# A two-layer cross-attention and FFN kernel on one core: its table of steps is put in another order

## The chip, the core and the metric

One core of a Trainium2 chip. The metric is the device time of one execution in microseconds (us), lower is better. The core has a matrix engine (TensorE, PE in the profile; PEld is its weight load), a vector engine (VectorE, DVE), an activation engine (ScalarE, ACT), a general engine (GpSimd, POOL) and an engine that only issues transfers here (SyncE, SP). Each runs its own instruction stream in order; they meet in semaphores.

## The reference

A batch of 2 sequences of 512 rows and 128 columns goes through four residual steps. Stage 0 and stage 2 are cross-attention to 77 context rows with 16 heads of 8 columns, stage 1 is an FFN with a small low-rank term chosen by expert, stage 3 a mixture of 8 experts (each row goes through one of them).

```python
x = x + xcond(layernorm(x), ctx, tau, delta, L0 weights)   # stage 0
x = x + lora_ffn(layernorm(x), L0 weights)                 # stage 1
x = x + xcond(layernorm(x), ctx, tau, delta, L1 weights)   # stage 2
x = x + switch_ffn(layernorm(x), L1 weights)               # stage 3

# xcond:  q = x@Wq.T+bq; k = ctx@Wk.T+bk; v = ctx@Wv.T+bv
#         a = softmax((q k * tau + delta)/sqrt(8)); out = (a v) @ Wo.T + bo
# lora_ffn: e = argmax(x@gate_W.T+gate_b)
#         out = relu(x@wi_W.T + wi_b + (x@A[e].T)@B[e].T) @ wo_W.T + wo_b
# switch_ffn: p = softmax(x@sw+sb); e = argmax p
#         out = (gelu(x@w1[e]+b1[e]) @ w2[e] + b2[e]) * p[e]
```

## The kernel before

Everything is in float32 and stays on the chip; 128 rows make a tile, so a batch has four tiles. The work is cut into some 280 named steps. `schedule()` holds one table of them; each engine's program is made by walking this same table and emitting that engine's share of each step, so the table alone sets the order on every engine. A step is `kind/layer/batch/number` (or `kind/stage/batch` for the four layer norms); `a:b` after the last number means from a to b-1. The kinds that matter here:

- `ln` and `xn`: layer norm statistics (VectorE L591, L594; ScalarE L494, L497) and the normalised rows `XN` (VectorE L603). `xt`: TensorE transposes them (L821), ScalarE copies them to `XNT` (L501), GpSimd adds a bias row to `X` meanwhile (L460).
- `kp/l`: the keys of layer l for both batches. TensorE L831 (8 instructions in the trace), ScalarE L509 and L516 (`Kf`, `Kt`), VectorE L625 (a copy `Ks<-Kt` that rounds) and L627. `km/l/b`: the masked copy `KG` of the keys, by VectorE for (0,0), by GpSimd L453 otherwise.
- `vp/l/b/j`: value projection, one matmul (L842, two instructions in the trace) and one VectorE operation (L643, `VP`).
- `q/l/b/g`: queries of head group g: TensorE L849, ScalarE L521, VectorE L648 (`QG`). `max/l/b/i`: TensorE L866 and a VectorE maximum L657 (`MR`). `mt/l/b/half`: the maxima are transposed (L875) and go into `QG` (ScalarE L526, VectorE L663). `sc/l/b/t`: scores, TensorE L891, exponential on ScalarE L534 (`P`, three buffers). `pv/l/b/t`: probabilities by values, TensorE L910. `on`, `ot`, `wo`: division, transposition and output projection (VectorE L670 and L675; TensorE L920, ScalarE L538; TensorE L927, VectorE L684).
- FFN 0: `gate/b` (TensorE L940, then on VectorE the six operations L695 to L706 and `U`, L715), `ut/b` (TensorE L948, VectorE L732 and L733; for b = 0 before them L728 and L729, which make `LS` from `LB`), `hid/b/0..3` (TensorE L953 and L957; the relu is on ScalarE L543 for even, on VectorE L738 for odd numbers), `out/b` (TensorE L967, VectorE L684).
- Stage 3: `route/b` and `prob/b` (TensorE L940, VectorE L695 to L708, ScalarE L548, VectorE L720 and L722), `rank/b` and `tiles/b` (TensorE L977 and L982, VectorE L747 to L765). After `rank/b` GpSimd scatters the four tiles of rows by expert to `slots` in HBM (L468), which needs the result of `rank` (`slot_ready`) and of `prob` (`p_ready`); SyncE then loads them back as `XS`. `moe/t` is the pipeline over 22 sorted tiles (11 of each batch): transposition of tile t+1 (L1004), first matmul of tile t (L1011), second of tile t-2 (L1022).

Two more things hold the steps together. The results of `xt`, `kp`, `q`, `vp`, `max`, `mt`, `gate` and others share four PSUM banks, given out in turn by `banks()` in the order of the table; a step waits for the reader of the bank's previous use. And GpSimd, which walks the same table, has little to do: it clears and fills constants for stage 3 where it meets `km/1/0`, which in both tables comes right after its part of `xt/1/0` in its own order:

```python
def moe_constants():
    finish(pool.memset(XS[:, :, :], 0.0), blank)              # L435
    ...
for s in steps:
    if s == ("km", 1, 0):
        moe_constants()
    if s[0] == "km" and s != ("km", 0, 0):
        pool.wait_ge(k_split, l + 1)                          # after L627 of kp/l
        ...
        for odd in (0, 1):
            finish(pool.tensor_tensor(*masked_k(b, odd), ALU.mult), kg_pool)
```

Of the kernel before, what the change touches and what calls it, by code (L numbers as in the profile page):

```python
# [96 lines left out]
def schedule():  # L97

    table = """
        ln/0/0 xn/0/0 delta xt/0/0 kp/0 q/0/0/0 km/0/0 q/0/0/1:4 max/0/0/0:3 km/0/1 vp/0/0/0 max/0/0/3:8 vp/0/0/1:4
        mt/0/0/0 vp/0/0/4 max/0/0/8 sc/0/0/0 ln/0/1 xn/0/1 max/0/0/9:11 pv/0/0/0 sc/0/0/1 max/0/0/11 vp/0/1/0 pv/0/0/1
        xt/0/1 sc/0/0/2 max/0/0/12 sc/0/0/3 vp/0/1/1 q/0/1/0 max/0/0/13:15 pv/0/0/2:4 max/0/0/15 sc/0/0/4 mt/0/0/1
        pv/0/0/4 max/0/1/0 vp/0/1/2 sc/0/0/5 max/0/1/1 q/0/1/1 vp/0/1/3 q/0/1/2 max/0/1/2:4 pv/0/0/5 vp/0/1/4  # L110
        max/0/1/4 sc/0/0/6 max/0/1/5 sc/0/0/7 q/0/1/3 pv/0/0/6:8 sc/0/0/8 max/0/1/6 sc/0/0/9 pv/0/0/8 max/0/1/7:10
        pv/0/0/9 on/0/0 mt/0/1/0 ot/0/0 sc/0/1/0 max/0/1/10:14 sc/0/1/1 wo/0/0 max/0/1/14 pv/0/1/0 sc/0/1/2 ln/1/0
        pv/0/1/1 vp/1/0/0 sc/0/1/3 xn/1/0 max/0/1/15 kp/1 pv/0/1/2 xt/1/0 mt/0/1/1 sc/0/1/4 gate/0 vp/1/0/1:3
        pv/0/1/3:5 sc/0/1/5:7 ut/0 pv/0/1/5 vp/1/0/3 hid/0/0:2 vp/1/0/4 hid/0/2 sc/0/1/7 hid/0/3 pv/0/1/6 vp/1/1/0
        out/0 vp/1/1/1 km/1/0 sc/0/1/8 pv/0/1/7 sc/0/1/9 ln/2/0 xn/2/0 pv/0/1/8:10 xt/2/0 vp/1/1/2 on/0/1 q/1/0/0:2
        vp/1/1/3 max/1/0/0:2 q/1/0/2 ot/0/1 max/1/0/2:7 wo/0/1 max/1/0/7 vp/1/1/4 ln/1/1 xn/1/1 mt/1/0/0 q/1/0/3
        xt/1/1 max/1/0/8 sc/1/0/0:2 max/1/0/9:11 gate/1 pv/1/0/0 max/1/0/11 pv/1/0/1 max/1/0/12:14 ut/1 max/1/0/14:16
        sc/1/0/2 hid/1/0 km/1/1 sc/1/0/3 hid/1/1:4 pv/1/0/2 mt/1/0/1 out/1 sc/1/0/4 pv/1/0/3 sc/1/0/5 pv/1/0/4 ln/2/1
        sc/1/0/6 xn/2/1 pv/1/0/5 sc/1/0/7 xt/2/1 pv/1/0/6 q/1/1/0:3 sc/1/0/8 max/1/1/0 pv/1/0/7 max/1/1/1:4 sc/1/0/9
        pv/1/0/8 max/1/1/4:8 pv/1/0/9 on/1/0 mt/1/1/0 max/1/1/8:10 q/1/1/3 sc/1/1/0 ot/1/0 max/1/1/10 pv/1/1/0 wo/1/0  # L120
        sc/1/1/1 max/1/1/11:14 sc/1/1/2 max/1/1/14 pv/1/1/1 sc/1/1/3 max/1/1/15 pv/1/1/2 mt/1/1/1 pv/1/1/3 sc/1/1/4:6
        ln/3/0 xn/3/0 pv/1/1/4 sc/1/1/6 pv/1/1/5 sc/1/1/7 xt/3/0 route/0 prob/0 pv/1/1/6:8 sc/1/1/8 rank/0 sc/1/1/9
        tiles/0 pv/1/1/8:10 on/1/1 ot/1/1 wo/1/1 ln/3/1 xn/3/1 moe/-1 xt/3/1 moe/0 route/1 moe/1 rank/1 tiles/1 prob/1
    """
# [984 lines left out]
```

## Time and profile before

| | before |
|---|---|
| time, median of 3 executions | 224.57 us (222.85 to 227.26) |
| span of the profiled execution, first to last instruction | 223.3 us |
| PE busy | 180.6 us (81%) |
| DVE busy | 140.4 us (63%) |
| ACT busy | 93.1 us (42%) |
| POOL busy | 62.9 us (28%) |
| mean granted TensorE clock | 0.908 of full speed |

The span is that of one profiled execution and is 1.3 us under the median of the unprofiled ones. Busy times are of instructions on the engine; an engine that is idle waits for a semaphore or issues. The granted clock is TensorE's clock as a share of 2.4 GHz; 0.5 is its lower level, 1.2 GHz. Times within the span count from its first instruction.

### The profile page before, as it was taken

How to read it: one execution, taken by the hardware profiler on the slowest of the kernel's cores; microseconds unless marked ns; L12 is line 12 of the kernel's file. 1: busy time of each engine (PE TensorE's matmuls, PEld its weight loads, DVE VectorE, ACT ScalarE, POOL GpSimd, SP SyncE). 2: the span in 40 equal slices, each digit the busy share in tenths (PEclk: the TensorE clock that was granted, in tenths of full speed). 3: DMA queues.
4: the chain of work that ended last, by engine and by line, in shares of the span. 5: the costliest groups of instructions: out<-in, count | busy, mean ns of one | idle time of the engine just before them, and what ended most of it. 6: DMA issues, size and time to landing. Idle time of an engine off the chain costs nothing.

```text
span 223.3 us, 3676 instructions
## 1 busy us (share of the span) xinstructions
PE 180.6 (81%) x1157; PEld 150.3 (67%) x1157; DVE 140.4 (63%) x385; ACT 93.1 (42%) x180; POOL 62.9 (28%) x68
## 2 busy tenths in 40 slices
...
DMA packets 11983, 15.43 MB, mean 69 GB/s; under 512 B 1713, under 2 KB 8898, under 8 KB 11965
## 3 DMA queue, kind: packets, MB, share of 16 engines
...
q8 instruction: 10, 0.16, 0.3%
...
## 4 chain that ended last, share of the span: by engine, by line
PE 42%; DVE 15%; issue 6%; ACT 4%; DMA 2%; POOL 2%; another core or an unknown queue 1%; DVEq 0%; ACTq 0%; POOLq 0%
PE scores L1011 8%; PE acc L1022 7%; PE acc L910 6%; PE shared L953 3%; PE shared L967 3%; PE shared L849 3%; DVE Ks L625 2%; PE scores L891 2%; PE shared L866 2%; PE shared L940 2%; DVE XN L603 2%; PE shared L821 1%; PE shared L1004 1%; DMA slots<-ROW,slot 1%; DVE stats L591 1%
## 5 line engine op out<-in xcount | busy, mean ns | idle before, releaser
L910 PE MATMUL acc<-VP,P 123*128 123x128 f32 (+1 forms) x320 | 42.9, 281 | 2.0 <-ACT P L534 2.0
L910 PEld LDWEIGHTS acc<-VP,P 123*128 123x128 f32 (+1 forms) x320 | 40.5, 195 | 5.2 <-ACT P L534 2.8
L534 ACT ACTIVATE P<-scores 123x512 f32<-123x512 f32 (+1 forms) x40 | 23.2, 595 | 36.5 <-PE scores L891 36.5
L460 POOL TENSOR_TENSOR X<-X,ROWS 128x512 f32<-128x512 f32 x6 | 8.1, 1352 | 86.2 <-DVE XN L603 86.1
L657 DVE TENSOR_REDUCE MR<-shared 128x4 f32<-128x308 f32 x64 | 27.1, 471 | 4.4 <-PE shared L866 3.8
L1011 PE MATMUL scores<-XST,HT 128*128 128x128 f32 x176 | 26.9, 303 | 3.4 <-ACT XST L564 3.4
L1011 PEld LDWEIGHTS scores<-XST,HT 128*128 128x128 f32 x176 | 24.7, 216 | 4.2 <-ACT XST L564 3.9
L474 POOL DMA_INDIRECT out<-XS,token x22 | 21.4, 974 | 20.1 <-DVE XS L789 17.2
L779 DVE TENSOR_TENSOR HT<-scores,B 128x512 f32<-128x512 f32 x22 | 15.2, 692 | 15.7 <-PE scores L1011 13.2
L1022 PE MATMUL acc<-W,HT 128*128 x176 | 24.9, 289 | 0.2 <-DVE XS L789 0.2
L866 PE MATMUL shared<-KG,QG 98*128 98x308 f32 x64 | 20.6, 384 | 5.1 <-DVE QG L648 4.0
L1022 PEld LDWEIGHTS acc<-W,HT 128*128 128x128 f32 x176 | 23.0, 205 | 0.4 <-issue 0.4
L891 PE MATMUL scores<-QG,KG 102*123 102x512 f32 (+1 forms) x48 | 19.6, 446 | 3.2 <-issue 2.9
L468 POOL DMA_INDIRECT slots<-ROW,slot x8 | 8.0, 1002 | 46.5 <-issue 46.5
L569 ACT ACTIVATE HT<-HT 128x512 f32<-128x512 f32 x22 | 13.9, 630 | 14.5 <-DVE HT L779 7.5
L866 PEld LDWEIGHTS shared<-KG,QG 98*128 98x128 f32 x64 | 12.0, 201 | 10.1 <-DVE QG L648 6.2
L648 DVE SCALAR_TENSOR_TENSOR QG<-shared,ATT,QG 32x512 fp32r<-32x512 f32 x16 | 11.8, 747 | 8.8 <-ACT QG L521 8.3
L849 PE MATMUL shared<-XNT,ATT 128*96 128x512 f32 x32 | 16.0, 615 | 0.9 <-issue 0.5
L562 ACT ACTIVATE HT<-W 128x512 f32 x22 | 13.8, 629 | 1.3 <-issue 1.0
L521 ACT ACTIVATE QG<-shared,ATT 96x512 fp32r<-96x512 f32 x16 | 10.8, 682 | 7.3 <-PE shared L849 7.3
L526 ACT ACTIVATE QG<-shared 6x512 fp32r<-6x512 f32 x8 | 4.7, 585 | 17.5 <-PE shared L875 17.5
L891 PEld LDWEIGHTS scores<-QG,KG 102*123 102x123 f32 (+1 forms) x48 | 8.3, 186 | 5.4 <-issue 3.6
...
## 6 DMA issues: line engine op xcount, KB each, us to landing
...
```

The source lines that it names most:

```text
L474: pool.indirect_dma_start(out, bass.IndirectOffsetOnAxis(ap=token[:, t:t + 1], axis=0), XS[:, t, 0:D], None, bounds_check=B * S - 1, oob_i ...
L534: act.activation(P[0:w, n % NP], scores[n % 2][0:w, :], ACT.Exp).then_inc(probs_ready, 1)
L562: act.activation(W1C[:, n % 2], W1[:, bass.ds(expert * F, F)], ACT.Identity).then_inc(w1_ready, 1)
L569: act.activation(HG1[:, t % NHB], HB[:, t % 2], ACT.Gelu_apprx_tanh).then_inc(gelu_ready, 1)
L657: dve.tensor_reduce(MR[:, b, qt, g, 2:2 + HG], bank(s)[:, 0:GK].rearrange("p (h k) -> p h k", h=HG), AX.X, ALU.max).then_inc(max_read, 1)
L779: dve.tensor_tensor(HB[:, t % 2].rearrange("p (k n) -> p k n", k=NF), hidden[t % 2][:, :].rearrange("p (k n) -> p k n", k=NF), bias, ALU.a ...
L849: pe.matmul(bank(s)[0:QR, :], ATT[l][:, A_Q + QR * g:A_Q + QR * (g + 1)], XNT[:, b], start=True, stop=True).then_inc(full[use[s][0]], 1)
L866: pe.matmul(bank(s)[:, 0:GK], QG[0:ONES + 2, b, g, 128 * qt:128 * qt + 128], KG[0:ONES + 2, b, g, off:off + GK], start=True, stop=True).th ...
L891: ins = pe.matmul(scores[n % 2][0:w, :], KG[:, b, g, c:c + w], QG[:, b, g], start=(i == 0), stop=(i == len(parts) - 1))
L910: ins = pe.matmul(acc[qt // 2][:, c:c + VW], P[0:w, n % NP, 128 * qt:128 * qt + 128], VP[0:w, l, b, j, half], start=(t == 0 and qt % 2 == ...
L1011: ins = pe.matmul(hidden[t % 2][:, 128 * k:128 * (k + 1)], W1C[:, t % 2, 128 * k:128 * (k + 1)], XST[:, t % 2], start=True, stop=True)
L1022: ins = pe.matmul(acc[n % 2][:, 0:D], HG1[:, n % NHB, 128 * k:128 * (k + 1)], W2[:, bass.ds(expert[n] * (NF * D) + D * k, D)], start=(k == ...
```

## The change

Only the table in `schedule()` is different. The set of steps, their instructions and all sizes are the same; what each engine does first and what later is not. Two of its lines, from the middle and the end:

```diff
-        pv/0/1/3:5 sc/0/1/5:7 ut/0 pv/0/1/5 vp/1/0/3 hid/0/0:2 vp/1/0/4 hid/0/2 sc/0/1/7 hid/0/3 pv/0/1/6 vp/1/1/0
+        sc/0/1/4 mt/0/1/1 vp/1/0/3 sc/0/1/5 gate/0 pv/0/1/4 vp/1/0/4 sc/0/1/6 pv/0/1/5 sc/0/1/7:9 ut/0 kp/1 hid/0/0:4
...
-        tiles/0 pv/1/1/8:10 on/1/1 ot/1/1 wo/1/1 ln/3/1 xn/3/1 moe/-1 xt/3/1 moe/0 route/1 moe/1 rank/1 tiles/1 prob/1
+        moe/-1 xn/3/1 xt/3/1 route/1 prob/1 moe/0:2 rank/1 tiles/1
```

What moves: `vp/0/0/0` and `kp/0` stand ahead of `xt/0/0`; `km/0/1` comes after `xt/0/1`; the value projections of batch 1 and of layer 1 come earlier; `kp/1` goes from between `xn/1/0` and `xt/1/0` to after `ut/0`; `ot/0/0` has seven steps between itself and `on/0/0`, where it had one; `wo/0/1` comes two maxima and one query step earlier; `out/1` is followed by fewer score and value steps; `km/1/1` comes after `xt/2/1`; `xt/3/0`, `route/0` and `rank/0` come earlier among the value steps; `route/1` and `prob/1` come ahead of `moe/0`.

The names of an instruction's row are output <- inputs. In the changed file every line number is one higher.

VectorE, FFN 0 of batch 0, from the normalised rows of stage 1 (`XN`) on, before:

```order
L603 TENSOR_SCALAR XN<-X,mean_var,rstd 128x128 x4
L657 TENSOR_REDUCE MR<-shared 128x4
L625 CAST Ks<-Kt 96x616
L627 TENSOR_TENSOR Ks<-Kt,Ks 32x616
L663 CAST QG<-shared 6x512
L695 TENSOR_TENSOR lg<-shared,ROWS 128x32
L696 TENSOR_REDUCE lmax<-lg 128x4
L698 TENSOR_TENSOR eq<-lg,lmax 128x32
```

The same place in the changed kernel. Ahead of the first row shown stand `XN`, two maxima, two value operations with `L664 CAST QG` between them, and the first two operations of the gate (`lg`, `lmax`):

```order
L699 TENSOR_TENSOR eq<-lg,lmax 128x32
L704 TENSOR_TENSOR eq<-eq,CON 128x32
L705 TENSOR_REDUCE first<-eq 128x4
L707 TENSOR_TENSOR hot<-eq,first 128x32
L716 TENSOR_TENSOR U<-shared,hot 128x4x32 x3
L644 TENSOR_TENSOR VP<-shared,CON 123x2x8x8
L729 CAST LS<-LB 96x512
L730 TENSOR_TENSOR LS<-LB,LS 32x512
L733 CAST U<-shared 96x512
L734 TENSOR_TENSOR U<-shared,U 32x512
L626 CAST Ks<-Kt 96x616
L628 TENSOR_TENSOR Ks<-Kt,Ks 32x616
```

The rounding copy `Ks<-Kt` stood two rows behind `XN`, ahead of the gate; it now stands behind the whole gate and the `U` work, right ahead of the odd relus of `hid`.

TensorE, FFN 0 of batch 1, from `out/1` (`W,HT`) to the queries (`XNT,ATT`) of layer 1, before:

```order
L967 MATMUL shared<-W,HT 128x128 x16
L891 MATMUL scores<-QG,KG 123x512
L910 MATMUL acc<-VP,P 128x128 x4
L891 MATMUL scores<-QG,KG 123x512
L910 MATMUL acc<-VP,P 128x128 x4
L891 MATMUL scores<-QG,KG 123x512
L910 MATMUL acc<-VP,P 128x128 x4
L891 MATMUL scores<-QG,KG 124x512 x2
L821 MATMUL shared<-CON,XN 128x128 x4
L910 MATMUL acc<-VP,P 128x128 x4
L849 MATMUL shared<-XNT,ATT 96x512 x3
```

The same place in the changed kernel:

```order
L968 MATMUL shared<-W,HT 128x128 x16
L892 MATMUL scores<-QG,KG 123x512
L911 MATMUL acc<-VP,P 128x128 x4
L892 MATMUL scores<-QG,KG 123x512
L892 MATMUL scores<-QG,KG 124x512 x2
L911 MATMUL acc<-VP,P 128x128 x4
L822 MATMUL shared<-CON,XN 128x128 x4
L892 MATMUL scores<-QG,KG 123x512
L850 MATMUL shared<-XNT,ATT 96x512 x3
```

Between `out/1` and the transposition stand two value steps (x4) where there were three and one score step fewer; between the transposition and the queries stands one score step where a value step was.

VectorE, the routing of batch 1, before, from the last operations of `rank/1` over `tiles/1` to `prob/1` (`esum`, and the reciprocal into `ROW`):

```order
L754 TENSOR_TENSOR place<-place,hot 128x32
L755 TENSOR_REDUCE slot_f<-place 128x4
L756 TENSOR_SCALAR slot<-slot_f 128x4
L761 TENSOR_TENSOR end_tile<-first_tile,tiles_of 1x8
L763 TENSOR_TENSOR past<-CON,end_tile 1x88
L764 TENSOR_REDUCE tile_f<-past 1x11
L765 TENSOR_SCALAR tile_e<-tile_f 1x11
L720 TENSOR_REDUCE esum<-ex 128x4
L722 RECIPROCAL ROW<-esum 128x4
```

In the changed kernel, from the end of `route/1` (`hotb`) over `prob/1` to the bias addition (`HT<-scores,B`) of `moe/0`, which is followed by that of `moe/1` and by `rank/1`:

```order
L709 CAST hotb<-hot 128x32
L721 TENSOR_REDUCE esum<-ex 128x4
L723 RECIPROCAL ROW<-esum 128x4
L774 TENSOR_LOAD tile_e
L774 ISA x2
L780 ISA
L780 TENSOR_TENSOR HT<-scores,B 128x512
```

`prob/1` stood last of all, behind `tiles/1`; it now stands right behind `route/1`, and both are ahead of the work on the first sorted tile.

## Rows read from the trace of the kernel before

**Rows 1.** Windows: length, busy PE, PEld, DVE, ACT, POOL (x), clock, DMA, GB/s.
```profile
57.72:86.80 29.08, 22.31 (x142) 18.67 (x140) 17.96 (x37) 7.37 (x15) 9.89 (x9) 0.88 0.31 101
62.80:69.00 6.20, 0.74 (x4) 0.33 (x3) 5.90 (x14) 1.08 (x2) 4.86 (x7) 0.79 0.67 228
69.00:73.60 4.60, 4.60 (x17) 3.77 (x18) 2.92 (x7) 0.00 (x0) 0.00 (x0) 0.54 1.07 329
...
160.90:172.00 11.10, 10.70 (x53) 10.22 (x54) 5.23 (x24) 8.69 (x15) 0.00 (x0) 0.50 0.36 116
```
**Rows 2.** Timeline of POOL: start, us, engine, line, instruction, shapes, count.
```profile
58.70 4.87 POOL L435 MEMSET XS<- 128x5720 f32 x1
...
65.50 2.57 POOL L453 TENSOR_TENSOR KG<-Ks,CON 102x616 fp32r<-102x616 f32 x2
```
**Rows 3.** Timeline of DVE, start of the kernel and FFN 0 of batch 0.
```profile
12.72 0.48 DVE L625 CAST Ks<-Kt 96x616 fp32r<-96x616 f32 x1 [0.64 <-ACT Kt L516]
...
14.84 2.70 DVE L633 TENSOR_TENSOR KG<-Ks,CON 102x616 fp32r<-102x616 f32 x2
...
56.12 1.11 DVE L603 TENSOR_SCALAR XN<-X,mean_var,rstd 128x128 f32<-128x128 f32 x4 [0.24 <-ACT rstd L497]
...
58.89 5.00 DVE L625 CAST Ks<-Kt 96x616 fp32r<-96x616 f32 x1 [1.27 <-ACT Kt L516]
63.93 0.79 DVE L627 TENSOR_TENSOR Ks<-Kt,Ks 32x616 fp32r<-32x616 f32 x1
...
65.92 0.86 DVE L698 TENSOR_TENSOR eq<-lg,lmax 128x32 f32<-128x32 f32 x1
66.81 0.19 DVE L703 TENSOR_TENSOR eq<-eq,CON 128x32 f32<-128x32 f32 x1
...
77.84 0.75 DVE L738 TENSOR_SCALAR HT<-shared,W 128x512 f32<-128x512 f32 x1 [1.92 <-PE shared L957]
```
**Rows 4.** Timeline of ACT, the keys of layer 1.
```profile
56.56 1.22 ACT L509 ACTIVATE Kf<-shared,ATT 96x154 f32<-96x154 f32 x4
57.86 1.00 ACT L516 ACTIVATE Kt<-Kf,tau 96x308 f32<-96x308 f32 x2
```
**Rows 5.** Timeline of PE, `ot/0/0` and the keys of layer 1.
```profile
49.92 0.63 PE L920 MATMUL shared<-CON,ON 128*128 128x128 f32 x4 [1.10 <-DVE ON L675]
...
55.77 1.22 PE L831 MATMUL shared<-CTX,ATT 128*96 128x154 f32 x8
```
**Rows 6.** Chain that ended last, in order of time: start, us, engine, output, line.
```profile
75.16 0.86 PE shared L953 x2
76.02 0.23 PE shared L957
76.25 0.46 PE scores L891 x2
...
77.80 0.89 PE acc L910 x8
...
78.92 3.65 PE shared L967 x32
...
86.80 0.63 PE shared L821 x4
...
114.24 3.59 PE shared L967 x32
...
121.86 0.63 PE shared L821 x4
```
**Rows 7.** Timeline of DVE, end of `rank/1` and of `prob/1`.
```profile
170.35 0.17 DVE L756 TENSOR_SCALAR slot<-slot_f 128x4 int32<-128x4 f32 x1
...
171.43 0.18 DVE L722 RECIPROCAL ROW<-esum 128x4 f32<-128x4 f32 x1
```
**Rows 8.** Timeline, `route/1` on ACT and the first scatter of batch 1 on POOL.
```profile
165.91 1.28 ACT L548 ACT_TABLE_LOAD   x1
...
172.85 0.97 POOL L468 DMA_INDIRECT slots<-ROW,slot  x1 [15.68 <-issue]
```

More of the change, by code:

```diff
@@ L106, in schedule @@
     table = """
[L107 to L111, printed above, removed]
@@ L112, in schedule @@
-        pv/0/0/9 on/0/0 mt/0/1/0 ot/0/0 sc/0/1/0 max/0/1/10:14 sc/0/1/1 wo/0/0 max/0/1/14 pv/0/1/0 sc/0/1/2 ln/1/0
-        pv/0/1/1 vp/1/0/0 sc/0/1/3 xn/1/0 max/0/1/15 kp/1 pv/0/1/2 xt/1/0 mt/0/1/1 sc/0/1/4 gate/0 vp/1/0/1:3
-        pv/0/1/3:5 sc/0/1/5:7 ut/0 pv/0/1/5 vp/1/0/3 hid/0/0:2 vp/1/0/4 hid/0/2 sc/0/1/7 hid/0/3 pv/0/1/6 vp/1/1/0
-        out/0 vp/1/1/1 km/1/0 sc/0/1/8 pv/0/1/7 sc/0/1/9 ln/2/0 xn/2/0 pv/0/1/8:10 xt/2/0 vp/1/1/2 on/0/1 q/1/0/0:2
-        vp/1/1/3 max/1/0/0:2 q/1/0/2 ot/0/1 max/1/0/2:7 wo/0/1 max/1/0/7 vp/1/1/4 ln/1/1 xn/1/1 mt/1/0/0 q/1/0/3
@@ L117, in schedule @@
[L117 to L121, printed above, removed]
@@ L122, in schedule @@
-        ln/3/0 xn/3/0 pv/1/1/4 sc/1/1/6 pv/1/1/5 sc/1/1/7 xt/3/0 route/0 prob/0 pv/1/1/6:8 sc/1/1/8 rank/0 sc/1/1/9
-        tiles/0 pv/1/1/8:10 on/1/1 ot/1/1 wo/1/1 ln/3/1 xn/3/1 moe/-1 xt/3/1 moe/0 route/1 moe/1 rank/1 tiles/1 prob/1
+        ln/0/0 xn/0/0 delta vp/0/0/0 kp/0 xt/0/0 km/0/0 q/0/0/0:3 max/0/0/0 q/0/0/3 vp/0/0/1 max/0/0/1:5 vp/0/0/2
+        max/0/0/5:8 vp/0/0/3:5 vp/0/1/0 max/0/0/8 mt/0/0/0 max/0/0/9 vp/0/1/1 sc/0/0/0 max/0/0/10 vp/0/1/2 sc/0/0/1
+        ln/0/1 xn/0/1 sc/0/0/2 pv/0/0/0:2 vp/0/1/3 max/0/0/11:13 pv/0/0/2 xt/0/1 max/0/0/13 sc/0/0/3 km/0/1 max/0/0/14
@@ new lines, in schedule @@
+        sc/0/0/4 max/0/0/15 vp/0/1/4 q/0/1/0 pv/0/0/3 mt/0/0/1 q/0/1/1 vp/1/0/0 pv/0/0/4 sc/0/0/5 q/0/1/2 sc/0/0/6
+        pv/0/0/5 max/0/1/0:3 pv/0/0/6 sc/0/0/7 max/0/1/3:5 q/0/1/3 max/0/1/5:7 sc/0/0/8:10 pv/0/0/7 max/0/1/7:9
+        pv/0/0/8 max/0/1/9 mt/0/1/0 max/0/1/10 pv/0/0/9 on/0/0 max/0/1/11 sc/0/1/0:2 max/0/1/12:14 vp/1/0/1 sc/0/1/2
+        ot/0/0 pv/0/1/0 wo/0/0 ln/1/0 pv/0/1/1 xn/1/0 max/0/1/14:16 pv/0/1/2 sc/0/1/3 pv/0/1/3 xt/1/0 vp/1/0/2
+        sc/0/1/4 mt/0/1/1 vp/1/0/3 sc/0/1/5 gate/0 pv/0/1/4 vp/1/0/4 sc/0/1/6 pv/0/1/5 sc/0/1/7:9 ut/0 kp/1 hid/0/0:4
```

9 lines of the change are left out of this document (added).

## The prediction

> **What bounds the kernel now.** I read the busy times of the engines first: TensorE is at work for 81% of the span, no other engine for more than 63%. So the end moves with TensorE's idle time and with its clock, and a table that only reorders can win nothing else. The windows tell where the idle time lies, and one stretch stands out: from the transposition of the stage-1 rows of batch 0 (`xt/1/0`, 57.72) to the one of stage 2 (`xt/2/0`, 86.80) pass 29.1 us [rows 1]. In 6.2 us of it, from 62.80 on, TensorE works 0.74 us, and in the 4.6 us after that its granted clock is 0.54, most of it at the lower of its two levels [rows 1].
>
> What holds it there is one VectorE instruction. `Ks<-Kt` (L625) starts at 58.89 and takes 5.00 us; the same copy takes 0.48 us for layer 0 [rows 3]. GpSimd clears `XS` from 58.70 to 63.57 [rows 2]: the copy ends 0.3 us after the clearing. The two overlap over the whole of it, so I read the 4.5 us as waiting. Behind the copy stand, in VectorE's order, L627, the maxima for `QG` that the next scores need, and the gate, on which `ut` and `hid` of TensorE wait. The rows of the chain show the work that follows: `hid`, `out/0`, the layer norm, `xt/2/0` [rows 6].
>
> **The stretch in the new order.** I count from the start of `xt/1/0`. In the old trace `XN` ends at 57.23 [rows 3], and the clearing starts 1.47 us later [rows 2]. In the new order TensorE waits for `XN` and starts about 0.16 us behind it, so the clearing runs from 1.3 to 6.2. GpSimd's own order is the same there, so this doesn't move.
>
> TensorE: `xt` 0.63; a value projection 0.2, a score step 0.23 [rows 6], four transpositions of maxima 0.45. VectorE's cast of the maxima (0.7, as an operation of 512 columns) ends at 2.25; another score step, then the gate, eight matmuls, about 0.9 like the eight of a value step [rows 6]: 3.4. VectorE: six operations at 0.22 from start to start (0.19 and the gap) [rows 3], 4.75, three for `U` 0.7, 5.45, one value projection 5.7. Then comes the copy `LS<-LB`, of the same kind as `Ks<-Kt` and smaller (under 0.48 [rows 3]). It meets the clearing until 6.2 and ends at 6.6. Three operations at 0.7 to 0.8, the first of them beside GpSimd's small copies: 8.9. That is when `U` is there.
>
> TensorE meanwhile: two value steps at 0.89 and three score steps (0.23, one of them 0.46) [rows 6], a value projection: 6.3. `ut` 0.45, the eight matmuls of `kp/1` 1.06 net (1.22 with overlap [rows 5]), the first half of `hid/0` 0.43: 8.25. It waits 0.65 for `U`. Then 0.23 and three times 0.66 (0.43 and 0.23 [rows 6]) and a score step: 11.35.
>
> `kp/1`, moved here, costs ScalarE 1.22 for `Kf` and 1.00 for `Kt` [rows 4]: from 7.4 to 9.7 with the wait for the last matmuls. VectorE follows with 0.48 and 0.79 [rows 3], 11.05, and behind these two wait both odd relus of `hid` at 0.75 [rows 3]: 12.55. So `out/0` starts at 12.6, a new wait of 1.2 us that the move makes. From the start of `out/0` to `xt/2/0` are 7.9 us in the old trace [rows 6], through the addition and the layer norm; TensorE's filler there, four value steps and two projections beside the 3.65 of `out/0`, fits in it (7.6). `xt/2/0` starts at 20.5: 29.1 - 20.5 = **8.6 us less**.
>
> Is the content the same? Between the two transpositions TensorE has the same steps as before, but that one value step and one value projection (1.1 us) now lie ahead of them and the eight matmuls of `kp/1` (1.06) among them; summed at the full clock both orders hold about 17.8 us. So the stretch doesn't win by leaving work outside it.
>
> **What surrounds it.** `xt/1/0` itself: TensorE's 1.10 us wait for `ON` ahead of `ot/0/0` [rows 5] is filled by 1.8 us of steps; but between `wo/0/0` and `xt/1/0`, where a chain of about 4.3 us runs (addition, layer norm), now stand only three value steps, two maxima and a score step, 3.3 us. One wait of 1.1 goes, one of 1.0 comes: 0.
>
> `xt/2/1`: from the end of `out/1` (114.24 + 3.59) to `xt/2/1` at 121.86 are 4.0 us [rows 6], filled by three value steps and four score steps. The new order leaves two value and three score steps, 0.89 x 2 + 0.23 x 2 + 0.46 = 2.7: a wait of 1.3. Between `xt/2/1` and the queries a score step stands for a value step, and the queries wait for `XNT` some 0.4 longer. **1.7 us more.**
>
> The routing of batch 1: the slots are ready at 170.52, `prob/1` at 171.61 [rows 7], the scatter starts at 172.85 [rows 8]. With `prob/1` ahead the scatter follows the slots: 1.1 less. One reload of ScalarE's table (1.28 [rows 8]) falls away for `route/1`, and another behind it. Against this the exponential of `route/1` now stands ahead of ScalarE's copies for tile 1 and waits for the gate logits, and TensorE waits 0.65 for `XNT` with no tile to work on: 0.8 more by my count. **0.3 us less.**
>
> The start of the kernel: `XNT` of batch 0 now stands behind `Kf` and `Kt` on ScalarE, at most 2.2 later [rows 4]; against it GpSimd no longer writes masked keys beside VectorE's two (2.70 [rows 3], and 0.79 each where nothing reads beside them): up to 1.1 less. VectorE is the engine that is waited for there. I take 0, and keep -1.1 and +2.2. Value projections and `km/1/1`, moved elsewhere, stand where TensorE is full in both orders, or far ahead of their reader: 0.
>
> Sum: -8.6 + 1.7 - 0.3 = -7.2. The profiled execution spans 223.3, 1.3 under the median of the runs; so a span of 216.1, and **217.4 us** as a median.
>
> **A price that the trace of before doesn't show.** Does an operation of VectorE with two inputs in SBUF wait for a clearing too? `eq<-lg,lmax` (L698) takes 0.86 at 65.92, beside GpSimd's `KG` product, whose first half ends at 66.8, and its like 0.19 [rows 2, 3]. GpSimd reads there. A clearing reads nothing, and in this trace no such VectorE operation meets one. From below 0; from above the whole gate waits until 6.2: `U` at 11.1, `out/0` at 13.95 for 12.6, 1.4 more. I take 0, since the only rows with a stretched product have a reading GpSimd.
>
> The Trainium skill (SBUF, State Buffer, section Who interferes with whom) says the same split: copies and casts in the two-port mode block with any GpSimd operation for its whole length, products with two SBUF inputs only with one that reads. By that rule the sum stays -7.2; if products waited too it would be -5.8.
>
> **The rivals.**
> The first: products wait for the clearing as well, as above: 217.4 + 1.4 = 218.8. For it: the product beside `KG`. Against it: GpSimd reads there.
>
> The second: the stall goes, but the clock takes part of it back. The new order makes waits of 1.0, 0.65, 1.2 and 1.3 us. In the old trace the clock was low after 6.2 us with little work, for 4.6 us [rows 1]; that costs 4.6 x 0.46 = 2.1. One or two such spells give 219.5 to 221.6. Against it: my waits are short beside that.
>
> The third, slower: the same mechanism in its long form. After the wait for the slots, 160.90 to 172.00 ran at 0.50 [rows 1], 11.1 us, which costs 5.5. The gain of 7.2 is used up when 14.4 us more run at the low clock; two long spells, at `out/0` and at `xt/2/1`, cost 11.1: 217.4 + 11.1 = 228.5. For it: full use there before, waits now. Against it: both spells of the trace come behind long idleness, and my waits are 1.3 us at most.
>
> The fourth: the change does little. The rest of the table, 87 to 150, is packed anew too; waits of 5 us in all that I don't see would leave 222.4. Such waits need a step that is short of filler; I found only the one at `xt/2/1`.
>
> **How the numbers follow.** The forecast with its bounds (start -1.1 to +2.2, a us for the filler) is 214.5 to 219.5: 0.52. Products wait: 0.10. Short spells of low clock: 0.16. Hidden waits: 0.13. Slower by the long spells: 0.09. The range 214.0 to 222.5 takes in all but the last and the ends of two others. More than 2%, about what a measurement of this kernel can tell, is under 220.1: the first two cases, and a quarter of the next two, 0.68. Within 2%: 0.24. Slower: 0.08.
>
> **What would show it.** In the new profile: `Ks<-Kt` of layer 1 at 0.5 us; `LS<-LB` longer than 0.5, ending with the clearing of `XS`; L699 at 0.19 within the clearing (0.86 or more speaks for the first rival); `xt/1/0` to `xt/2/0` at 20 to 21 us; granted clock 1.0 there; a new wait of TensorE ahead of `out/0` with VectorE's `HT` as releaser, and one ahead of `xt/2/1`; one table load less on each side of `route/1`. The prediction is wrong if VectorE reaches `LS<-LB` long before the clearing ends, if the clock stays low, or if 87 to 150 grows by more than 2 us.

## The result and the profile after

| | before | changed |
|---|---|---|
| time, median of 4 executions each | 224.42 us (222.85 to 227.26) | 215.54 us (214.40 to 216.53) |
| ratio, 95% interval | | 0.963 (0.9567 to 0.9694) |
| span of the profiled execution | 223.3 us | 214.7 us |
| PE / DVE / ACT / POOL busy | 180.6 / 140.4 / 93.1 / 62.9 us | 177.7 / 133.5 / 90.5 / 62.3 us |
| mean granted clock | 0.908 | 0.935 |

The changed kernel is 3.7% faster. The forecast was 217.4 us, the sum behind it 7.2 us off the span; the span lost 8.6. Times here and below are medians of all executions, but ratios are of the fast ones alone, those within 1.5% of the kernel's fastest (left out are one of 216.02 us in e1, one of 432.06 in e5, one of 219.04 in e6 and two of 228.6 of the kernel before), so that a ratio need not be the quotient of the two times. The windows of the changed kernel come first: the stretch from `xt/1/0` to `xt/2/0`, then the same clock times as the second row of [rows 1], then two places of which more is said below. Columns as in [rows 1]; the last but two is the granted clock.

```profile
55.60:77.18 21.58, 19.96 (x139) 16.75 (x138) 12.32 (x38) 8.54 (x18) 9.86 (x9) 1.00 0.43 137
62.80:69.00 6.20, 5.62 (x21) 3.12 (x19) 4.13 (x6) 3.88 (x9) 2.24 (x4) 1.00 1.02 336
109.00:118.00 9.00, 6.94 (x30) 4.11 (x29) 3.80 (x14) 4.25 (x9) 3.72 (x3) 0.84 0.01 2
152.00:163.00 11.00, 9.36 (x44) 8.23 (x45) 4.24 (x19) 6.19 (x12) 0.00 (x0) 0.50 0.39 120
```

The stretch took 29.08 us at a clock of 0.88 [rows 1] and now takes 21.58 at 1.00. From 62.80 to 69.00 TensorE works 5.62 us where it worked 0.74.

GpSimd's timeline has the clearing as long as before [rows 2]:

```profile
56.76 4.87 POOL L436 MEMSET XS<- 128x5720 f32 x1
```

It runs to 61.63. VectorE's timeline beside it and behind it (start, duration, in brackets the idle time before the instruction and its releaser):

```profile
59.33 0.19 DVE L696 TENSOR_TENSOR lg<-shared,ROWS 128x32 f32<-128x32 f32 x1 [1.20 <-PE shared L941]
...
59.78 0.19 DVE L699 TENSOR_TENSOR eq<-lg,lmax 128x32 f32<-128x32 f32 x1
60.01 0.19 DVE L704 TENSOR_TENSOR eq<-eq,CON 128x32 f32<-128x32 f32 x1
...
61.48 0.43 DVE L729 CAST LS<-LB 96x512 fp32r<-96x512 f32 x1
...
63.51 0.69 DVE L734 TENSOR_TENSOR U<-shared,U 32x512 fp32r<-32x512 f32 x1
65.72 0.48 DVE L626 CAST Ks<-Kt 96x616 fp32r<-96x616 f32 x1 [1.51 <-ACT Kt L517]
66.23 0.79 DVE L628 TENSOR_TENSOR Ks<-Kt,Ks 32x616 fp32r<-32x616 f32 x1
67.05 0.75 DVE L739 TENSOR_SCALAR HT<-shared,W 128x512 f32<-128x512 f32 x1
68.22 0.75 DVE L739 TENSOR_SCALAR HT<-shared,W 128x512 f32<-128x512 f32 x1 [0.42 <-PE shared L958]
```

The whole gate lies beside the clearing at 0.19 an operation. `Ks<-Kt` takes 0.48 where it took 5.00 [rows 3], and the copy that the forecast put into the clearing, `LS<-LB`, meets only its last 0.15 us.

TensorE's timeline shows the new waits: before `xt/1/0`, before `sc/0/1/5`, before `out/0`, and two around `xt/2/1`:

```profile
54.60 1.16 PE L911 MATMUL acc<-VP,P 123*128 123x128 f32 x8 [0.93 <-ACT P L535]
...
57.98 0.49 PE L892 MATMUL scores<-QG,KG 102*123 102x512 f32 x1 [0.68 <-ACT QG L527]
...
69.12 1.13 PE L968 MATMUL shared<-W,HT 128*128 128x128 f32 x8 [0.70 <-DVE HT L739]
...
113.16 0.63 PE L822 MATMUL shared<-CON,XN 128*128 128x128 f32 x4 [1.56 <-DVE XN L604]
...
114.52 4.48 PE L850 MATMUL shared<-XNT,ATT 128*96 128x512 f32 x6 [0.50 <-issue]
```

And the routing of batch 1, in the timelines of VectorE (`prob/1`, then the slots), ScalarE and GpSimd:

```profile
158.28 0.18 DVE L723 RECIPROCAL ROW<-esum 128x4 f32<-128x4 f32 x1
...
158.88 1.28 ACT L570 ACT_TABLE_LOAD   x1
...
163.37 0.17 DVE L757 TENSOR_SCALAR slot<-slot_f 128x4 int32<-128x4 f32 x1
...
164.75 0.97 POOL L469 DMA_INDIRECT slots<-ROW,slot  x1 [16.08 <-issue]
```

Cut at the same five steps, the two spans differ as follows (`ot/1/1` is the last transposition of attention, at 153.42 before and 145.62 after):

| section | before | after | measured | forecast |
|---|---|---|---|---|
| start to `xt/1/0` | 57.72 | 55.60 | -2.1 | 0 |
| `xt/1/0` to `xt/2/0` | 29.08 | 21.58 | -7.5 | -8.6 |
| `xt/2/0` to `ot/1/1` | 66.62 | 68.44 | +1.8 | +1.7 |
| `ot/1/1` to first scatter of batch 1 | 19.43 | 19.13 | -0.3 | -0.3 |
| first scatter to the end | 50.45 | 49.95 | -0.5 | 0 |
| sum | 223.3 | 214.7 | -8.6 | -7.2 |

### The profile page after: what moved, and what is told of

Same layout as the page of the kernel before. It is cut to its first block, busy times and chain, and to the rows that moved or that the text cites. A ratio compares the mean times of both kernels' runs of the same rounds, so it can differ in the third digit from the quotient of the medians.

```text
span 214.7 us, 3672 instructions
## 1 busy us (share of the span) xinstructions
PE 177.7 (83%) x1157; PEld 144.8 (67%) x1157; DVE 133.5 (62%) x385; ACT 90.5 (42%) x178; POOL 62.3 (29%) x68
## 4 chain that ended last, share of the span: by engine, by line
PE 54%; DVE 22%; issue 7%; ACT 5%; DMA 4%; another core or an unknown queue 2%; POOL 2%; DVEq 1%; ACTq 0%; POOLq 0%
PE acc L911 10%; PE scores L1012 7%; PE acc L1023 6%; PE shared L850 5%; PE scores L892 4%; PE shared L968 3%; PE shared L954 3%; DVE MR L658 3%; PE shared L867 3%; DVE QG L649 2%; PE shared L941 2%; DMA X<-in_x 2%; DVE XN L604 2%; PE shared L822 2%
## 5 line engine op out<-in xcount | busy, mean ns | idle before, releaser
L911 PE MATMUL acc<-VP,P 123*128 123x128 f32 (+1 forms) x320 | 41.8, 276 | 0.9 <-ACT P L535 0.9
L911 PEld LDWEIGHTS acc<-VP,P 123*128 123x128 f32 (+1 forms) x320 | 39.8, 191 | 3.5 <-ACT P L535 2.0
L461 POOL TENSOR_TENSOR X<-X,ROWS 128x512 f32<-128x512 f32 x6 | 8.1, 1352 | 76.5 <-DVE XN L604 76.4
L1012 PE MATMUL scores<-XST,HT 128*128 128x128 f32 x176 | 26.4, 298 | 4.5 <-ACT XST L565 3.5
L1012 PEld LDWEIGHTS scores<-XST,HT 128*128 128x128 f32 x176 | 23.7, 210 | 6.2 <-ACT XST L565 4.7
L475 POOL DMA_INDIRECT out<-XS,token x22 | 21.4, 974 | 19.6 <-DVE XS L790 16.8
L1023 PE MATMUL acc<-W,HT 128*128 x176 | 23.2, 276 | 0.2 <-DVE XS L790 0.2
L850 PE MATMUL shared<-XNT,ATT 128*96 128x512 f32 x32 | 19.0, 710 | 4.9 <-DVE VP L644 3.1
L1023 PEld LDWEIGHTS acc<-W,HT 128*128 128x128 f32 x176 | 21.3, 192 | 0.4 <-issue 0.4
L850 PEld LDWEIGHTS shared<-XNT,ATT 128*96 128x96 f32 x32 | 5.5, 191 | 10.4 <-issue 10.4
```

What stands on the lines that cost most here:

```text
L475: pool.indirect_dma_start(out, bass.IndirectOffsetOnAxis(ap=token[:, t:t + 1], axis=0), XS[:, t, 0:D], None, bounds_check=B * S - 1, oob_i ...
L850: pe.matmul(bank(s)[0:QR, :], ATT[l][:, A_Q + QR * g:A_Q + QR * (g + 1)], XNT[:, b], start=True, stop=True).then_inc(full[use[s][0]], 1)
L911: ins = pe.matmul(acc[qt // 2][:, c:c + VW], P[0:w, n % NP, 128 * qt:128 * qt + 128], VP[0:w, l, b, j, half], start=(t == 0 and qt % 2 == ...
L1012: ins = pe.matmul(hidden[t % 2][:, 128 * k:128 * (k + 1)], W1C[:, t % 2, 128 * k:128 * (k + 1)], XST[:, t % 2], start=True, stop=True)
L1023: ins = pe.matmul(acc[n % 2][:, 0:D], HG1[:, n % NHB, 128 * k:128 * (k + 1)], W2[:, bass.ds(expert[n] * (NF * D) + D * k, D)], start=(k == ...
```

## The experiments

Theory: the gain is the copy that no longer waits for the clearing, and the smaller terms are as in the forecast. Against it: products wait too; the rest of the table does the work; the clock takes part back; the new waits at `xt/2/1` and in the routing cost what they show. Three sets of four kernels ran, each beside the kernel before on its own chip: that one took 219.05, 224.67 and 218.81 us. So sets are compared by their ratio to the kernel before, never in microseconds. Every measured ratio below has its 95% interval behind it.

**`e1_early_clear` and `e2_early_clear_new`: the clearing at another time, in the old and in the new table.** GpSimd clears `XS` at its part of `xt/0/1`, far ahead of FFN 0, and fills its other constants there too; nothing else differs.

```diff
-if s == ("km", 1, 0):
+if s == ("xt", 0, 1):
     moe_constants()
```

> The kernel before with one edit: GpSimd clears XS and fills the stage-3 constants at its part of xt/0/1 (about 19 to 24 us, where it is idle) and no longer right behind xt/1/0. The table is the old one. If the 5.00 us copy Ks<-Kt waits for the clearing (my theory), it falls to about 0.5 us, the gate comes 4.5 us earlier, and with the clock of the 4.6 us behind it (2.1 us) the kernel gains 4.5 to 6.5: 218 to 220. If the order itself was what held TensorE there (rival), the copy may get short but the time stays at 223 to 225.

> The changed kernel with the same edit (clearing at GpSimd's part of xt/0/1). In it nothing waited for the clearing (Ks<-Kt 0.48, LS<-LB 0.43, products 0.19), so my theory expects the same time within 0.5 us, 215 to 216. The rival, that some of VectorE's work still meets the clearing and waits unseen, expects 1 us or more less.

Old table with the early clearing: 213.20 us, ratio 0.9681 (0.9588 to 0.9774). Its timelines on GpSimd and VectorE:

```profile
19.76 4.87 POOL L435 MEMSET XS<- 128x5720 f32 x1
...
57.17 0.48 DVE L625 CAST Ks<-Kt 96x616 fp32r<-96x616 f32 x1 [1.27 <-ACT Kt L516]
```

Its window of the stretch:

```profile
56.00:78.34 22.34, 20.31 (x142) 16.83 (x140) 12.79 (x37) 7.36 (x15) 3.43 (x4) 1.00 0.00 1
```

The old order, untouched, falls from 29.08 to 22.34 when the clearing is elsewhere: 6.7 us, clock included. The stall was the clearing's, shown. The new table with the same edit: 210.32 us, 0.9624 (0.9541 to 0.9707), the same ratio as the changed kernel, and its stretch takes 21.59 us for 21.58; the new order has nothing left that the clearing holds up. The two cures don't add: the new table is worth 3.7% alone and about 0.6% on top of the early clearing, with intervals that overlap.

**`e3_kp_alone` and `e4_kp_back`: the keys of layer 1 alone.** In e3 the old table gets this one move; in e4 the new table loses it.

```diff
# e3, old table
-xn/1/0 max/0/1/15 kp/1 pv/0/1/2 xt/1/0 ... ut/0 pv/0/1/5
+xn/1/0 max/0/1/15 pv/0/1/2 xt/1/0 ... ut/0 kp/1 pv/0/1/5
# e4, new table
-max/0/1/14:16 pv/0/1/2 ... ut/0 kp/1 hid/0/0:4
+max/0/1/14:16 kp/1 pv/0/1/2 ... ut/0 hid/0/0:4
```

> The kernel before with one step moved: kp/1 stands behind ut/0, as in the changed one; all else in the old order. My theory: the copy is 0.5 us, the gate comes 4.5 us earlier; a wait of about 1 us at the odd relus of hid comes in its place; 218 to 220, so that most of the change's gain is this one move. Rival: the gain needs the other moves of the new table too; then 221 to 224.

> The changed kernel with kp/1 back at its old place (behind max/0/1/15, ahead of pv/0/1/2), all else new. My theory: Ks<-Kt meets the clearing again, takes about 5 us and holds the gate: 5 to 6.5 us more, 220.5 to 222. Rival (the other moves fill the stall with TensorE work): at most 3 more, under 218.5.

e3: 212.04 us, 0.9697 (0.9629 to 0.9765): the one move is worth 3.0 of the 3.7%. GpSimd and VectorE in e3:

```profile
56.92 4.87 POOL L435 MEMSET XS<- 128x5720 f32 x1
...
58.53 0.19 DVE L698 TENSOR_TENSOR eq<-lg,lmax 128x32 f32<-128x32 f32 x1
...
60.43 1.63 DVE L728 CAST LS<-LB 96x512 fp32r<-96x512 f32 x1
```

Here the step of the forecast that the changed kernel hardly shows is plain: `LS<-LB` starts 1.36 us before the clearing ends at 61.79, takes 1.63 for 0.43, and ends 0.27 behind it. A copy waits for the clearing, a product beside the same clearing takes 0.19. The windows of the stretch in e3 and in e4:

```profile
55.59:78.59 23.00, 21.22 (x148) 18.15 (x148) 13.55 (x38) 8.64 (x18) 10.03 (x9) 1.00 0.40 128
```
```profile
57.30:80.92 23.62, 20.41 (x131) 16.43 (x130) 11.93 (x34) 6.54 (x12) 6.94 (x8) 0.95 0.39 125
```

e4: 214.58 us, 0.9793 (0.9719 to 0.9868). Against e2 of the same set that is 1.7% of the kernel before, 3.7 us, where the stall's full price of 5 to 6.5 had been expected to come back. It did not, and e4's timelines of GpSimd and VectorE show why:

```profile
54.41 1.26 POOL L461 TENSOR_TENSOR X<-X,ROWS 128x512 f32<-128x512 f32 x1 [20.44 <-DVE XN L604]
55.73 5.08 POOL L436 MEMSET XS<- 128x5720 f32 x1
...
62.07 2.57 POOL L454 TENSOR_TENSOR KG<-Ks,CON 102x616 fp32r<-102x616 f32 x2
...
55.26 0.75 DVE L626 CAST Ks<-Kt 96x616 fp32r<-96x616 f32 x1 [0.22 <-ACT Kt L517]
...
62.47 0.87 DVE L699 TENSOR_TENSOR eq<-lg,lmax 128x32 f32<-128x32 f32 x1
```

In this order the copy starts 0.47 us ahead of the clearing, and now the clearing is the longer one, 5.08 for 4.87. The copy's own 0.27 too much falls on another GpSimd operation, the bias addition (L461), which ran until 55.67. The expectation had placed the keys in the table and taken the order of arrival for granted. By this trace, the only one of its kind here, the one that starts first goes through and the other pays, and a copy that pays has the whole of VectorE's queue behind it. So the 3.7 us of e4 are not the stall. Its trace shows three other things, which no run separates: `xt/1/0`, with the keys' matmuls ahead of it, comes later than in any other new order (57.30 for 53.6 to 56.2), the clock is at 0.58 from 57.30 to 60.00, and two gate operations (L699 above, and L707) take 0.87 beside GpSimd's product `KG`.

**`e5_new_to_xt10`, `e6_new_to_xt20`, `e7_new_to_out1`, `e8_new_to_on11`: the new table up to a step, the old order behind it.** All steps up to the named one (`xt/1/0`, `xt/2/0`, `out/1`, `on/1/1`) stand as in the new table; the steps left follow in the order of the old one.

```diff
# e5, behind xt/1/0
-xt/1/0 vp/1/0/2 sc/0/1/4 mt/0/1/1 vp/1/0/3 sc/0/1/5 gate/0
+xt/1/0 kp/1 mt/0/1/1 sc/0/1/4 gate/0 vp/1/0/2 pv/0/1/4 sc/0/1/5:7
# e8, behind on/1/1
-on/1/1 ot/1/1 tiles/0 wo/1/1 ln/3/1 moe/-1 xn/3/1 xt/3/1 route/1 prob/1 moe/0:2 rank/1 tiles/1
+on/1/1 tiles/0 ot/1/1 wo/1/1 ln/3/1 xn/3/1 moe/-1 xt/3/1 moe/0 route/1 moe/1 rank/1 tiles/1 prob/1
```

> New order up to xt/1/0, the rest in the old order (kp/1 comes first of the rest, and its copy meets the clearing as before). The trace of the changed kernel has xt/1/0 2.1 us earlier, where I had forecast 0. If that gain is real and lasts: 222.3. If it is only work put off (rival): 224.4.

> New order up to xt/2/0, the rest old. By the traces xt/2/0 is 9.6 us earlier; the rest as before. If the new rest costs 1.0 net (traces: -9.6 there, -8.6 at the end), this one is faster than the changed kernel: 214.8. If part of the 9.6 is work put off, it stands at 216 or above.

> New order up to out/1, the rest old, so that between out/1 and xt/2/1 and ahead of the queries the old filling stands. My step (two value and three score steps are short of filler there: 1.7 us, with the clock at its lower level for the queries) expects this one 1 to 1.7 us faster than the changed kernel, 214 to 214.5; if the wait is given back later anyway, the same as it.

> New order up to on/1/1, the rest old: tiles/0 stands where it did or ahead, route/1 behind moe/0, prob/1 last. My step says the new routing order is worth 0.3 us, so 215.8. If only the 1.1 us of prob/1 counts: 216.6. If the wait of TensorE for XNT (0.78 in the trace) weighs more: 215.0 or less.

| new order up to | time | ratio |
|---|---|---|
| `xt/1/0` (e5) | 222.52 us | 0.9922 (0.9873 to 0.9971) |
| `xt/2/0` (e6) | 216.12 us | 0.9660 (0.9571 to 0.9749) |
| `out/1` (e7) | 215.67 us | 0.9588 (0.9500 to 0.9675) |
| `on/1/1` (e8) | 214.35 us | 0.9531 (0.9472 to 0.9591) |

The front is worth 0.8%, 1.8 us, and the next cut brings the rest: e6 has the changed kernel's ratio, 0.966 and 0.963, so what the new order does behind `xt/2/0` comes to less than the interval. e6 was expected at 0.957 and e7 at 0.954 to 0.956; both came out higher, with intervals that reach down to what was expected. In e6's trace the clock fell at `ut/1`, and the section from `xt/2/0` to `ot/1/1` took 68.84 us for 66.62.

e7 doesn't test what its expectation says. Between `out/1` and `xt/2/1` it has the same three score and two value steps as the changed kernel, since `sc/1/0/4` and `pv/1/0/3` already stand ahead of `out/1`; only the layer norm stands earlier among them. The wait at `xt/2/1` is 1.33 us for 1.56. But e7 shows something else. Its section from `xt/2/0` to `ot/1/1` takes 68.10 us at a clock of 1.00, 1.4 more than the changed order does at that clock (66.7, below). GpSimd's, VectorE's and TensorE's timelines in e7:

```profile
92.17 2.52 POOL L454 TENSOR_TENSOR KG<-Ks,CON 102x616 fp32r<-102x616 f32 x2
...
93.78 0.96 DVE L699 TENSOR_TENSOR eq<-lg,lmax 128x32 f32<-128x32 f32 x1
...
96.28 0.61 PE L949 MATMUL shared<-CON,U 128*96 128x128 f32 x4 [1.04 <-DVE U L716]
```

With `km/1/1` at its old place GpSimd's product runs beside `gate/1`: L699 takes 0.96 us, and TensorE waits 1.04 for `U`. In the changed kernel, where `km/1/1` comes after `xt/2/1`, L699 takes 0.19, and the wait is 0.28 in e9. That is 0.76 of the 1.4; the rest lies behind `xt/2/1`, where e7 takes 31.57 us to `ot/1/1`, as the old order does (31.56), and e9 30.77.

e5 repeats the stall in another size. `kp/1` stands behind `xt/1/0` there, the copy starts 2.46 us into the clearing, and VectorE's timeline has

```profile
59.11 2.73 DVE L626 CAST Ks<-Kt 96x616 fp32r<-96x616 f32 x1 [3.17 <-ACT Kt L517]
```

which ends at 61.84, 0.32 behind the end of the clearing at 61.52. The copy again waits out what is left of the clearing and ends 0.3 us behind it, as in the kernel before. The clock was low behind it here too (0.52 from 60 to 66), and the stretch takes 28.96 us, as long as the old one.

e8 was faster than the 215.8 expected, and lies where a greater weight of the `XNT` wait would have put it (215.0 or less); that wait, 0.78 in the changed kernel, isn't in e8's trace. From `ot/1/1` to the first scatter it took 18.0 us for 19.1, although its scatter waits for `prob/1` again (slots at 159.65, `prob/1` at 160.74, scatter at 161.98). In e8 the clock was 1.00 between two low spells, from 155 to 157; in the changed kernel it was 0.50 from 150 to 162. How much of the 1.1 us is order and how much clock, this run doesn't say.

**`e9_new_again`, `e10_prob_first`, `e11_rank_first`, `e12_filled`: the routing and the wait at `xt/2/1`.** e9 is the changed kernel. e10 has e8's routing with `prob/1` ahead of `rank/1`; e11 also `rank/1` ahead of `moe/1`; e12 is e11 with another filler around `xt/2/1`.

```diff
# e10 against e8
-moe/0 route/1 moe/1 rank/1 tiles/1 prob/1
+moe/0 route/1 moe/1 prob/1 rank/1 tiles/1
# e11 against e10
-moe/0 route/1 moe/1 prob/1 rank/1 tiles/1
+moe/0 route/1 prob/1 rank/1 moe/1 tiles/1
# e12 against e11
-sc/1/0/5 pv/1/0/4 sc/1/0/6:8 ln/2/1 xn/2/1 pv/1/0/5 xt/2/1 sc/1/0/8 q/1/1/0:3
+sc/1/0/5 pv/1/0/4 sc/1/0/6 pv/1/0/5 sc/1/0/7 ln/2/1 xn/2/1 sc/1/0/8 pv/1/0/6 xt/2/1 pv/1/0/7 q/1/1/0:3
```

> The changed kernel itself once more, beside the three that follow. 0.960 to 0.966 of the kernel before. By the traces so far its clock either stays high after the 1.5 us wait ahead of xt/2/1 (two of five new-order traces) or falls, and then on/1/1 comes 1.7 us later; so its profile may have 66.7 or 68.4 us from xt/2/0 to ot/1/1.

> New order up to on/1/1, old routing order behind it (route/1 behind moe/0), but prob/1 ahead of rank/1 instead of last. In the run before this one without that move the slots were ready at 159.65 and the scatter waited for prob/1 until 161.98. If the scatter hangs on prob/1 there (my step of 1.1 us), it now follows the slots by 1.1 to 1.3 us, 1.0 us earlier than without; 0.950 of the kernel before. If not, 0.955.

> As e10, and rank/1 ahead of moe/1. TensorE waits 3.4 us for batch 1's sorted rows at the end of batch 0's, so an earlier rank/1 should move the end: slots ready 1.5 to 2.5 us earlier, batch 0's tiles half a microsecond later, and 1.5 to 2 us off the total, 0.943 to 0.948. Rival: batch 0's tiles then end last, and the gain is under 0.7.

> As e11, and between out/1 and the queries of layer 1 for batch 1 stand four value steps and the score steps of the old order, taken from behind the queries. My step: the 1.55 us wait ahead of xt/2/1 goes under 0.3 and the clock doesn't fall there; if the wait is what costs, 1 to 1.7 us less than e11; if the work is only missed later, among the maxima, the same time as e11 when that one's clock stays high.

| | time | ratio | `ot/1/1` to first scatter | `ot/1/1` to the end |
|---|---|---|---|---|
| e9 | 210.46 us | 0.9626 (0.9539 to 0.9712) | 19.1 | 65.3 |
| e10 | 210.13 us | 0.9603 (0.9519 to 0.9688) | 16.8 | 63.0 |
| e11 | 210.00 us | 0.9636 (0.9551 to 0.9721) | 16.5 | 64.2 |
| e12 | 210.41 us | 0.9642 (0.9549 to 0.9735) | 17.0 | 64.5 |

e10 and e11 missed the times expected of them; e11's rival, a gain under 0.7, is what came. In e10 the scatter follows the slots by 1.2 us, as put, and comes 2.3 us earlier than in e9; in e11 it comes 2.6 earlier. The times stay within 0.5 us of each other, though intervals of 0.9% either way would hide a gain of 1 us, and the profiled executions are 0.9 to 2.4 us shorter than e9's behind `ot/1/1`; e10's clock was also low there for less time than e9's. The reason why an earlier scatter brings so little can be read in the changed kernel, in the timelines of SyncE (the load of batch 1's rows) and TensorE (the transposition of the twelfth sorted tile, the first of batch 1):

```profile
171.07 1.85 SPq L400 DMA_DIRECT2D XS<-slots  x4
...
182.43 0.27 PE L1005 MATMUL shared<-CON,XS 128*128 128x128 f32 x1
```

The first of these loads (130 KB, 2.2 us in the median from issue to landing) is in by 173.3, some 9 us before its rows are used. In e9 the load is issued at 168.96 for a use at 176.54, in e11 at 166.12 for 175.25. In e11 the sorted tiles follow each other at 1.9 us without a wait from 161.96 on, so rows that land earlier are only there earlier. The expectation of e11 took a wait of TensorE at the seventh sorted tile for one for these rows; more of it at the end.

Now the wait at `xt/2/1`. e12 gave TensorE the value step and the filler back and kept a wait of 1.29 us. ScalarE's timeline in e12 tells why:

```profile
111.49 0.60 ACT L535 ACTIVATE P<-scores 124x512 f32<-124x512 f32 x1 [0.76 <-PE scores L892]
111.98 0.29 ACT L495 ACTIVATE logvar<-mean_var,eps 128x4 f32<-128x4 f32 x1
```

and the same two rows in the changed kernel:

```profile
110.28 1.09 ACT L535 ACTIVATE P<-scores 123x512 f32<-123x512 f32 x2 [0.53 <-PE scores L892]
111.26 0.30 ACT L495 ACTIVATE logvar<-mean_var,eps 128x4 f32<-128x4 f32 x1
```

In both, `ln/2/1` comes behind `sc/1/0/7`. Its first ScalarE operation waits there for exponentials whose scores TensorE makes only after its value steps. The mean and variance are complete at 110.85 in e12 and 111.01 in the changed kernel; `logvar` starts 1.13 and 0.25 us later. In the kernel before, where `ln/2/1` stands behind `sc/1/0/5`, it started 0.03 us after them. From the start of the addition to that of `XN` pass 2.68 us before, 2.90 in the changed kernel and 3.77 in e12. So of the 1.56 us some 0.2 is a longer chain and the rest is missing filler. e7 bears this out: with the same filler and the layer norm where the old order has it, the chain is 2.68 and the wait 1.33. e12 put the filler back, but a score step too far ahead of the layer norm, and lengthened the chain by the 1.1 us that it had filled.

What the wait costs is another matter. The section from `xt/2/0` to `ot/1/1` in windows of the kernel before, of the changed kernel and of e9, which is the same program as the changed one:

```profile
86.80:153.42 66.62, 56.81 (x363) 44.45 (x364) 44.78 (x133) 25.45 (x47) 7.45 (x6) 1.00 0.00 1
```

```profile
77.18:145.62 68.44, 58.76 (x364) 45.20 (x364) 43.78 (x132) 25.70 (x47) 7.92 (x7) 0.98 0.01 2
```
```profile
76.82:143.57 66.75, 57.18 (x363) 44.60 (x364) 43.77 (x132) 25.67 (x47) 7.89 (x7) 1.00 0.01 2
```

and the queries behind the wait in e9's timeline, with the same 1.56 us ahead of them:

```profile
112.80 0.63 PE L822 MATMUL shared<-CON,XN 128*128 128x128 f32 x4 [1.56 <-DVE XN L604]
...
114.16 2.79 PE L850 MATMUL shared<-XNT,ATT 128*96 128x512 f32 x6 [0.50 <-issue]
```

In e9, e2, e4, e11 and e12, at the full clock, the section takes 66.7 us, 0.1 more than in the old order's 66.62 (66.64 in e3 and e5). TensorE's idle time there is 66.62 - 56.81 = 9.8 us before and 66.75 - 57.18 = 9.6 in e9: the wait came, and other waits of the section shrank by as much. They are not given back by themselves: in e7, where the old order follows `out/1`, the wait is nearly as long and the section 1.4 us longer. In the changed kernel's profile, in e8 and in e10 the clock fell behind the wait, the six query matmuls took 4.3 to 4.5 us for 2.79, and it takes 68.3 to 68.4. The old order has its own low spells: in e1 and e6 the clock fell at `ut/1`, and the section took 68.9 and 68.8.

## Why the prediction was right, step by step

**The stall.** Right, and shown by e1, e3 and e5. The copy of the old order waits out the clearing, the 4.5 us come back, and the 4.6 us of low clock behind them too. The stretch gained 7.5 for 8.6. In every trace that has the new order there it takes 21.56 to 21.60 us, so the forecast's 20.5 was off by a real 1.1. In its own steps: `U` was there at 8.6 us after `xt/1/0` (8.9 forecast); `out/0` started at 13.5 (12.6), with a wait of 0.70 ahead of it (1.2), and the rest took 8.06 (7.9). Of the 0.9 ahead of `out/0` most is one wait that the count left out: `sc/0/1/5` waited 0.68 for `QG`, the cast behind the transposed maxima, and TensorE's steps behind it came later by that. `Kf` waited for the matmuls of `kp/1` and started at 7.8 for 7.4, `Kt` ended at 10.1 for 9.7, and the last odd relu waited another 0.42 for the matmuls of `hid`, which the forecast had ready by then. The order of the chain (`Kt`, `Ks`, both odd relus, `out/0`) is as it was put.

**Products beside the clearing.** The 0 was right: 0.19 for L699 inside the clearing here and in e3. The Trainium skill (SBUF — State Buffer, section Who interferes with whom) states this split, and the traces agree on both sides: the copy of 0.43 took 1.63 beside the clearing in e3, and a product of 0.19 took 0.96 beside GpSimd's reading `KG` product in e7. The first rival is refuted; its 1.4 us are nowhere.

**`xt/1/0` itself, put at 0, measured -2.1.** This is the term that failed, by its size. The forecast let the wait for `ON` go and a wait of 1.0 come; the first fell from 1.10 [rows 5] to 0.17, and the second is there with 0.93. But the old order's own waits of value steps for probabilities ahead of `xt/1/0` went too, which I had not counted. They are, in TensorE's timeline of the kernel before:

```profile
26.69 1.13 PE L910 MATMUL acc<-VP,P 123*128 123x128 f32 x8 [0.49 <-ACT P L534]
28.75 1.16 PE L910 MATMUL acc<-VP,P 123*128 123x128 f32 x8 [0.32 <-ACT P L534]
...
45.90 1.16 PE L910 MATMUL acc<-VP,P 123*128 123x128 f32 x8 [0.30 <-ACT P L534]
```

That is 1.1 us, and 0.43 ahead of transposed maxima and 0.34 ahead of a maximum went with them; the 0.93 is the only wait of more than 0.2 left. The windows from the first `mt/0/0` to `xt/1/0`, before and changed:

```profile
23.51:57.72 34.21, 30.98 (x204) 25.74 (x203) 23.86 (x69) 15.76 (x31) 1.61 (x2) 0.97 0.05 17
```
```profile
24.12:55.60 31.48, 30.11 (x202) 25.58 (x201) 22.69 (x67) 14.26 (x27) 3.89 (x4) 0.96 0.01 4
```

TensorE's idle time there fell from 3.2 to 1.4 us and its work by 0.9. The old order takes 34.0 to 34.2 in three traces, the new one 30.9 to 31.5 in seven and 32.6 to 32.9 in e10 to e12, where the clock was low at the beginning of this window. In the mean 0.8 us is paid back at the start, where `mt/0/0` comes that much later. `xt/1/0` moves by some 2 us from trace to trace in either order, 55.6 to 57.7 in the old and 53.6 to 56.2 in the new (e4 apart), so the -2.1 of one pair is about right and not exact: the means differ by 1.6, and e5, whose stretch is as long as the old one, gives -1.8 as a time. The start's bounds (-1.1 to +2.2) didn't reach that far, since they were made from the keys alone.

**`xt/2/1`, put at +1.7, measured +1.8.** The number agrees and the reason does not. The wait came as forecast, 1.56 for 1.3, yet e9 has it and loses 0.1, since the idle time of the whole section is no longer than before; I had priced the wait and not asked what the rest of the section gives back. e7 shows where 1.4 of it comes from: the new order behind `xt/2/1`, and `km/1/1`, whose move I had put at 0 and which is worth 0.76 there. That the steps taken out of the gap fill other gaps agrees with e12, which moved them back for nothing. What cost 1.7 in the profiled execution is the clock behind the wait, which is the second rival in one spell (its price was 2.1). So the agreement is luck: the term is right in size here by a mechanism that I had given 0.16.

**The routing, -0.3, measured -0.3.** The scatter follows the slots by 1.2 us and no longer `prob/1`; the slots come 0.8 later after `ot/1/1` (17.9 for 17.1), both as put; of three table loads from 163 on one is left. But the table cuts the time at the scatter, and nothing waits for the scatter: batch 1's rows lay ready some 9 us early. The step took an earlier scatter for time won. That the number is met says little for it, and e11, with a scatter 2.6 us earlier, gained at most a part of that.

**The slower rival and the hidden waits** didn't occur. No long spell followed the waits at `out/0` and `xt/2/1`; the long one of the old order, at the first sorted tiles, is there as before, 0.50 from 152 to 163. The argument against that rival, that both low spells of the old trace come behind long idleness, had overlooked one at the start, 0.55 from 18 to 24. The fourth rival's place, 87 to 150, holds the value that it had.

So the forecast was met with 1.4 us to spare, because the front, 2.1 better, and the last section, 0.5 better, outweighed a stretch 1.1 worse; the last section's 0.5 is less than the change of one wait there, 3.25 us before and 2.30 after, whose cause stays open (more of it at the end). One step carries the result, and it is the one shown by undoing its cause.
